# Two-layer graph network on one core: stores of the first groups moved to GpSimd's queue, four of eleven row tables on VectorE, the last norm by tiles between row parts, the last product by rows with its stores on two queues

## The reference, cut to what matters

```python
xn = layernorm(x)
x = x + rgcn_gate(xn, edges, types) + performer_attention(xn)     # layer 0
x = x + quantised_ffn(layernorm(x))
xn = layernorm(x)
x = x + gcn(xn, edges) + linear_attention(xn)                     # layer 1
# the last part, which the change touches most:
h = layernorm(x)
probs = sigmoid(h @ Wr.T + rb)                # 8 experts, best 2 kept, as weights cw
out = expert_shared(h)                        # silu(h Wg.T) * (h Wu.T) @ Wd.T
for e in range(8): out = out + cw[..., e:e+1] * expert_e(h)
x = x + out
```

## Time and profile before

| | |
|---|---|
| median of three runs | 2032.35 us |
| the profiled execution | 2033.57 us |
| its span, first to last instruction | 2032.1 us |
| TensorE busy, mean granted clock | 92% of the span, 0.958 |
| VectorE, GpSimd, ScalarE busy | 54%, 35%, 22% |
| DMA moved | 162.63 MB, mean 80 GB/s |

### The profile page before, as it was taken

One profiled execution on the slowest core, in us unless ns is written; L12 is line 12 of the kernel. 1 busy time (PEld: TensorE's weight loads), 2 busy tenths in 40 slices (PEclk: granted clock), 3 DMA queues, 4 the chain that ended last, 5 costly groups with the idle time before them and its releaser, 6 DMA issues.

```text
span 2032.1 us, 28436 instructions
## 1 busy us (share of the span) xinstructions
PE 1861.5 (92%) x9601; PEld 1456.3 (72%) x9601; DVE 1089.6 (54%) x2672; ACT 452.1 (22%) x1044; POOL 712.1 (35%) x581
## 2 busy tenths in 40 slices
PE   6989899999999999999999997544999999979997
PEld 4865566666877878778787776443878888757776
DVE  7877799998354453544534289866522234241021
ACT  3149955552011010110101130121000011010010
POOL 2000000002534535345353568000566551526651
PEclk9999999999999999999999999755999999989999
DMA  4431122222412122121224341000244441112211
GB/s 137 142 109 58 65 72 68 73 88 75 136 51 77 52 64 83 48 77 52 66 80 142 106 133 59 15 32 6 93 149 149 127 132 34 53 36 74 77 57 56
DMA packets 109418, 162.63 MB, mean 80 GB/s; under 512 B 7563, under 2 KB 42313, under 8 KB 109060
## 3 DMA queue, kind: packets, MB, share of 16 engines
q1 hardware_dynamic: 76934, 123.36, 19.8%
q10 hardware_dynamic: 32094, 36.94, 5.5%
q0 software_dynamic: 288, 1.02, 0.2%
HBM read 136.01 MB, written 25.28 MB: 79 GB/s over the span
## 4 chain that ended last, share of the span: by engine, by line
PE 66%; DVE 9%; DVEq 2%; ACT 1%; issue 1%; ACTq 0%
PE ps L409 16%; PE ps L410 16%; PE ps L411 16%; PE ps L1235 8%; PE ps L2144 1%; PE ps L1200 1%; PE ps L1642 1%; DVE stats L313 1%; PE ps L1172 1%; PE ps L1145 1%; PE ps L871 1%; DVE x L1538 0%; DVE x L1482 0%; PE ps L2155 0%; PE ps L1210 0%
## 5 line engine op out<-in xcount | busy, mean ns | idle before, releaser
L409 PE MATMUL ps<-w_hi,xt_hi 128*125 128x512 f32 (+1 forms) x1800 | 753.0, 418 | 28.8 <-DVE ring L480 7.7
L249 POOL TENSOR_TENSOR w_hi<-w_stage,zero 128x512 fp32r<-128x512 f32 x280 | 314.3, 1123 | 1240.3 <-PE ps L411 736.2
L410 PE MATMUL ps<-w_lo,xt_hi 128*125 128x512 f32 (+1 forms) x1800 | 711.5, 395 | 0.0
L411 PE MATMUL ps<-w_hi,xt_lo 128*125 128x512 f32 (+1 forms) x1800 | 709.7, 394 | 0.0
L409 PEld LDWEIGHTS ps<-w_hi,xt_hi 128*125 128x125 f32 x1800 | 338.2, 188 | 107.7 <-issue 17.0
L411 PEld LDWEIGHTS ps<-w_hi,xt_lo 128*125 128x125 f32 x1800 | 337.4, 187 | 84.9
L252 POOL TENSOR_TENSOR w_lo<-w_stage,w_hi 128x512 fp32r<-128x512 f32 x280 | 387.2, 1383 | 21.9
L410 PEld LDWEIGHTS ps<-w_lo,xt_hi 128*125 128x125 f32 x1800 | 338.3, 188 | 69.9
L1235 PE MATMUL ps<-a_hi,xn_hi 125*128 125x313 f16 (+1 forms) x640 | 106.7, 297 | 1.0 <-DVE mtmp L1373 1.0
L1235 PE MATMUL ps<-a_hi,xn_lo 125*128 125x313 f16 (+1 forms) x640 | 106.3, 296 | 0.0
L1406 DVE TENSOR_TENSOR nat<-nat,ps 125x512 f32<-125x512 f32 x80 | 51.9, 684 | 94.7 <-PE ps L411 78.8
(11 more groups left out here) (366 smaller groups left out, 2052.8 us busy)
## 6 DMA issues: line engine op xcount, KB each, us to landing
w_stage<-in_stream SPq DMA_DIRECT2D x374, 256.0 KB, 2.7
pre<-ring ACTq DMA_DIRECT2D x75, 250.0 KB
a_qk<-pre SPq DMA_DIRECT2D x16, 312.5 KB
a_qkf<-pre ACTq DMA_DIRECT2D x14, 312.5 KB
a_vx<-pre SPq DMA_DIRECT2D x9, 312.5 KB
nat<-pre SPq DMA_DIRECT2D x2, 1250.0 KB
x<-in_x SPq DMA_DIRECT2D x5, 500.0 KB
z<-pre SPq DMA_DIRECT2D x2, 1250.0 KB
```

What stands on the lines that cost most here:

```text
L249: POOL.tensor_tensor(w_hi[:, q, :], w_stage[:, q % NST, :], zero[:].to_broadcast([128, 512]), ALU.add).then_inc(S("hi_done"), 1)
L409: PE.matmul(dst, l_hi, r_hi, start=first, stop=False)
L410: PE.matmul(dst, l_hi, r_lo, start=False, stop=False)
L411: return PE.matmul(dst, l_lo, r_hi, start=False, stop=last)
```

## The change

1. `store` leaves ScalarE; GpSimd issues the 45 stores of groups 0 to 8 behind its first eight chunks. The semaphores of the stores no longer start at 16.
2. `row_on_dve`: j % 3 == 1, that is j = 1, 4, 7 and 10 of the 11.
3. The last norm: the second projection group runs in passes over tiles (0, 1) and (2, 3, 4), the turns of tiles 0 and 1 inside the second pass; the first group of the experts in passes (0, 1), (2, 3), (4,), with the turns of tiles 2, 3 and 4, the router's halves and the turning of the logits between. `meet` and `ln_split` are gone; the `again_*` helpers become `tile_*` with other banks.
4. The last product: in the second half, expert 0 for all tiles, then tile by tile experts 1 to 8. The last tile is added and stored in two halves of 256 columns; stores alternate between SyncE's and ScalarE's queue.

```diff
+    for g in range(G_PRE0 - 1):
+        for m in range(T):
+            POOL.wait_ge(S("bank_free"), (g + 1) * T + m + 1)
+            POOL.dma_start(pre[g, m], ring[:, m, :]).then_inc(S(f"stpre0_{m}"), 16)
 ...
-        def store(g):
-            for m in range(T):
-                ALE.wait_ge(S("bank_free"), (g + g0 + 1) * T + m + 1)
-                ALE.dma_start(pre[bass.ds(g, 1), m].rearrange("a p f -> p (a f)"), ring[:, m, :]).then_inc(S(f"st{tag}_{m}"), 16)
 ...
-                DVE.wait_ge(S(f"st{tag}_{m}"), 16 * g + 16)
+                if g:
+                    DVE.wait_ge(S(f"st{tag}_{m}"), 16 * g)
 ...
     def row_on_dve(j):
-        return j % 4 == 3
+        return j % 3 == 1
 ...
+    def tile_banks(m, o):
+        if m % 2 == 0:
+            return (6, 7) if o == AGAIN else (5, 6)
+        return (4, 5) if o == AGAIN else (7, m)
 ...
+    def dense_part(c0, g0, rows, behind):
+        for k in range(KT):
+            PE.wait_ge(S("split_done"), NST + c0 + k + 1)
+            for m in rows:
+                if k == 0:
+                    PE.wait_ge(S("bank_free"), g0 * T + m + 1)
+                last = three(...)
+                ...
+            behind(k)
 ...
-    dense_pe(1, C_P1, G_P1)
+    def beside_last(k):
+        if k in (3, 5):
+            tile_turn(k // 4, LAST)
+    dense_part(C_P1 + KT, G_P1 + 1, (0, 1), lambda k: None)
+    dense_part(C_P1 + KT, G_P1 + 1, (2, 3, 4), beside_last)
 ...
-    meet()
-    ln_split(x1, nat)
 ...
+    for m in (0, 1):
+        proj1_evac(1, m)
+        tile_var(m, LAST)
+    for m in (0, 1):
+        tile_norm(m, LAST)
+        tile_high(m, LAST)
+    for m in (0, 1):
+        tile_low(m, LAST)
+    for m in (2, 3):
+        proj1_evac(1, m)
+        tile_var(m, LAST)
+    for m in (2, 3):
+        tile_norm(m, LAST)
+    proj1_evac(1, 4)
+    tile_var(4, LAST)
+    for m in (2, 3):
+        tile_high(m, LAST)
+        tile_low(m, LAST)
+    tile_norm(4, LAST)
+    tile_high(4, LAST)
+    router_copy(0)
+    tile_low(4, LAST)
+    router_copy(1)
 ...
+    def beside_up(rows):
+        def behind(k):
+            if rows[0] == 0 and k in (4, 6):
+                tile_turn(2 if k == 4 else 3, LAST)
+            if rows[0] == 2 and k == 0:
+                tile_turn(4, LAST)
+            if rows[0] == 2 and k == 3:
+                PE.wait_ge(S("x_low"), LAST + T)
+                router_pe(1)
+            if rows[0] == 2 and k == 6:
+                PE.wait_ge(S("logits"), 2)
+                ...
+        return behind
+    for rows in ((0, 1), (2, 3), (4,)):
+        PE.wait_ge(S("x_low"), LAST + rows[-1] + 1)
+        if rows[0] == 2:
+            router_pe(0)
+        if rows[0] == 4:
+            PE.wait_ge(S("logits"), 1)
+        dense_part(c0, g0, rows, beside_up(rows))
 ...
+    for e in range(NEXP + 1):
+        down_part(0, (e,), range(T))
+    down_part(1, (0,), range(T))
+    down_part(1, range(1, NEXP + 1), range(T))
 ...
+            cols = ((0, 512),) if (h, m) != (1, T - 1) else ((0, 256), (256, 512))
+            for f, (b, e) in enumerate(cols):
+                n_part[0] += 1
+                o = x1[:, m, h * 512 + b:h * 512 + e]
+                DVE.tensor_tensor(o, o, ps[0:P, m, b:e], ALU.add).then_inc(S("y_done"), 1)
+                eng = (ALE, SP)[n_part[0] % 2]
+                eng.wait_ge(S("y_done"), n_part[0])
+                eng.dma_start(y[m, :, h * 512 + b:h * 512 + e], o).then_inc(S("st_out"), 16)
```

More of the change, by code:

```diff
@@ L872, in hist_pe, with beside @@
                       skip_group_check=True)
-    def beside(dense, evacuate, load_bias, store):
+    def beside(dense, evacuate, load_bias):
         mk = bucket_counts(evacuate)
@@ L2197, in beside_proj1, with beside_again @@
             feed_pe(ao1, 4 + k, FEED1 + 4 + k)
[L2199 to L2214, removed]
+    tile_turn(0, AGAIN)
+    tile_turn(1, AGAIN)
+    def beside_again(rows):
+        def behind(k):
             if rows[0] == 0 and k in (1, 5):
-                again_turn(2 + k // 5)
+                tile_turn(2 + k // 5, AGAIN)
             if rows[0] == 0 and k == 2:
@@ L2219, in build @@
             if rows[0] == 2 and k == 1:
-                again_turn(4)
+                tile_turn(4, AGAIN)
+        return behind
+    for rows in ((0, 1), (2, 3), (4,)):
+        PE.wait_ge(S("x_low"), AGAIN + rows[-1] + 1)
+        PE.wait_ge(S("down_free"), 6 if rows[0] == 0 else 2 * T)
+        dense_part(c0, g0, rows, beside_again(rows))
     for g in range(1, G_PRE1):
@@ L2396, in build, with proj1_evac @@
     done["groups"] += G_PRE1 + 2
[L2398 to L2406, removed]
+    def proj1_evac(g, m):
+        wait_bank(DVE, g, m, C_P1, G_P1)
+        o = x1[:, m, g * 512:(g + 1) * 512]
+        DVE.tensor_tensor(o, o, ps[0:P, m, :], ALU.add).then_inc(S("bank_free"), 1)
         DVE.drain()
-        done["chunks"] += 2 * KT
-        done["groups"] += 2
+        stats_tile(x1, m, (g,))
+    done["chunks"] += 2 * KT
+    done["groups"] += 2
     wr = at("wr", [128, KT, NEXP], F32, R_EXTRA)
@@ L2435, in build, with router_pe @@
         DVE.tensor_copy(n[:, :, NODES:NP2], zero[:].unsqueeze(1).to_broadcast([128, KT, 1]))
-    mk_wr = sig(DVE.drain(), "dve_step")
-    meet()
-    ln_split(x1, nat)
-    wait(PE, mk_wr)
-    for i, (h0, hn) in enumerate(((0, 314), (314, 312))):
+    H_ROUTER = ((0, 314, 4), (314, 312, 7))
+    def router_pe(i):
+        h0, hn, bank = H_ROUTER[i]
         for k in range(KT):
-            t_ = three(ps[0:NEXP, 5 + i, 0:hn], wr_hi[:, k, :], wr_lo[:, k, :], xt_hi[:, k, h0:h0 + hn], xt_lo[:, k, h0:h0 + hn],
+            t_ = three(ps[0:NEXP, bank, 0:hn], wr_hi[:, k, :], wr_lo[:, k, :], xt_hi[:, k, h0:h0 + hn], xt_lo[:, k, h0:h0 + hn],
@@ L2446, in build, with router_copy @@
                        k == 0, k == KT - 1)
-        mk = sig(t_, "pe_step")
-        wait(DVE, mk)
-        mk_lg = sig(DVE.tensor_copy(lgt[:, h0:h0 + hn], ps[0:NEXP, 5 + i, 0:hn]), "dve_step")
+        t_.then_inc(S("router"), 1)
+    def router_copy(i):
+        h0, hn, bank = H_ROUTER[i]
+        DVE.wait_ge(S("router"), i + 1)
+        DVE.tensor_copy(lgt[:, h0:h0 + hn], ps[0:NEXP, bank, 0:hn]).then_inc(S("logits"), 1)
+    for m in (0, 1):
+        proj1_evac(1, m)
+        tile_var(m, LAST)
@@ L2453, in build, with behind @@
     c0, g0 = done["chunks"], done["groups"]
[L2455 to L2462, removed]
+    def beside_up(rows):
+        def behind(k):
+            if rows[0] == 0 and k in (4, 6):
[7 more added lines that the diff above has]
+                PE.wait_ge(S("logits"), 2)
+                for t in range(T):
+                    t_ = PE.transpose(ps[0:P, 5, t * NEXP:(t + 1) * NEXP], lgt[:, t * P:(t + 1) * P], ident[0:NEXP, 0:NEXP])
+                t_.then_inc(S("router"), 1)
+        return behind
@@ L2463, in build @@
+    for rows in ((0, 1), (2, 3), (4,)):
+        PE.wait_ge(S("x_low"), LAST + rows[-1] + 1)
[4 more added lines that the diff above has]
+        dense_part(c0, g0, rows, beside_up(rows))
     with PE.Fori(1, G_UP) as g:
         dense_pe(g, c0, g0)
-    DVE.wait_ge(S("router"), 1)
-    DVE.tensor_tensor(pr[:], ps[0:P, 7, 0:T * NEXP].rearrange("p (t e) -> p t e", t=T),
+    DVE.wait_ge(S("router"), 3)
+    DVE.tensor_tensor(pr[:], ps[0:P, 5, 0:T * NEXP].rearrange("p (t e) -> p t e", t=T),
@@ L2540, in build, with down_part @@
     y = out.rearrange("(t p) d -> t p d", p=P)
-    for h in range(2):
-        for e in range(NEXP + 1):
-            c = c0 + h * (NEXP + 1) + e
-            q = c % NSL
-            PE.wait_ge(S("split_done"), NST + c + 1)
-            for m in range(T):
+    def down_part(h, experts, rows):
+        for m in rows:
+            for e in experts:
+                c = c0 + h * (NEXP + 1) + e
+                q = c % NSL
+                if m == 0:
+                    PE.wait_ge(S("split_done"), NST + c + 1)
                 if e == 0:
```

154 lines of the change are left out of this document (59 added, 95 removed).

## The result

The changed kernel takes 1986.03 us (median of 4 runs, 1983.74 to 1987.83) where the kernel before takes 2032.67 (4 runs); ratio 0.9767, 95% interval [0.9755, 0.978]. That is 46.6 us less; 38.8 were forecast and 1993.6 us. The profiled execution took 1984.67 us with a span of 1983.3, 48.8 less than the span of before.

A forecast was written before the change was run, and what follows sets the result against it. TensorE was busy 92% of the span, so only its waits counted. Terms 9.3 + 8.9 − 1 + 15.4 + 6.2 = 38.8 took the profiled 2033.57 to 1994.8, the runs to 1993.6 us; range 1983 to 2008.

The forecast's parts named there:

- Row tables, 9.3: Scatter groups: ScalarE loses two scalings a step, so 6.14 us a step instead of 6.72, 16 × 0.58 = 9.3 us less.
- TensorE's 5.85: Scatter groups: TensorE would need about 5.85 us a step, so ScalarE still leads at 6.14.
- Stores, 8.9 less 1: Group ends: stores on GpSimd's queue free ScalarE's bias load and count copies, 8.9 us gained, 1 us lost to contention.
- The 1 us of contention: Scatter and histogram groups: GpSimd's store issues hold up VectorE, taken as 1 us from a range of nothing to 18.
- The fourth rival: More than computed: granted clock stays at 1.00 after waits, steps fall to 5.85; 9 us more, 1984 us; chance 0.12.
- Last norm, 15.4: End of first projection group to logits' slot given back: 84.9 us becomes 68.9, less 0.65 lost, 15.4 us gained.
- The third rival: Last norm late tile by tile through port waits and ScalarE's order, 2 us each, 10 less gained, 2003.6 us; chance 0.13.
- Last product, 6.2: Kernel's end: tail behind the last matmul 4.3 us instead of 10.8; gain 6.4, less 0.2 for halves, 6.2 us.
- First and second rival: First: VectorE paces scatter, ScalarE's 0.58 not had, 2002.9 us, chance 0.12. Second: GpSimd's stores slow VectorE's tables, 2038.6, 0.03.
- signs: What the trace would show, among it splits 6.1 us apart and no ScalarE idle over 3 us at group ends.

The follow-up runs named there:

- e6: The changed kernel with five row tables of eleven on VectorE (j = 1, 3, 5, 7, 9) instead of four: 1986.82 us, ratio 0.9769 to the kernel before.
- e9: The changed kernel with VectorE's low part of the chunk behind the tables of j = 7 instead of j = 4: 1980.3 us, ratio 0.9748 to the kernel before.
- e3: The kernel before, stores still on ScalarE's queue, those of the last scatter and three histogram groups spread one behind each count copy 3 to 7: 2022.47 us, ratio 0.9943.
- e2: The kernel before with only the stores of groups 0 to 8 moved to GpSimd's queue: 2016.37 us, ratio 0.9918.
- e4: The kernel before with the last product alone changed (second half tile by tile, stores on two queues, last one in halves): 2026.77 us, ratio 0.996.
- e7: The changed kernel with the last tile's two stores cut by rows, 112 on one queue and 13 on the other: 1985.61 us, ratio 0.9765 to the kernel before.
- e8: The changed kernel with the last tile added and stored in one piece of 512 columns: 1986.22 us.
- e1: The kernel before with the row tables alone changed (j = 1, 4, 7 and 10 on VectorE): 2024.83 us, ratio 0.9953.
- e5: The kernel before with the last norm alone changed (by tiles between the row parts): 2016.89 us, ratio 0.992.
- e11: The changed kernel with the low parts of the histogram groups' 32 chunks made by GpSimd instead of VectorE: 2007.19 us, ratio 0.9882 to the kernel before.

## Why the prediction came out as it did

Between the two profiled executions 48.8 us came off, 10.0 more than the 38.8. Of these, 6.2 are the stores, whose term was too small, and 3.2 lie in two stretches that the change does not touch.

- **Row tables, 9.3: right.** 6.13 us a step where 6.14 stood. The reason was half right. ScalarE led, but 0.64 us a step of VectorE's wait for the split, which I took for slack, was part of the loop that held ScalarE too (0.24 a step of its own waiting, before and after; the prediction had about 0.35). e6 and e9 showed it: moving one more scaling bought nothing, moving the wait bought 0.35 a step. TensorE's 5.85 was wrong, it can do 5.62.
- **Stores, 8.9 less 1: the mechanism right, the term too small.** By place: 1.2, 1.9, 0.5 against 1.5, 2.0, 0.9 measured; and the three ends of the histogram, 2.1, 1.6 and 1.6, against 4.0, 3.3 and 2.6 (from evacuation to evacuation, and from the last to the split at 478). The six add up to 14.3; the changed execution was 0.1 us behind when they began. The step that failed is "I take 2.1, 1.6 and 1.6, between the 1.06 of TensorE and 2.15 of VectorE": I read one wait of one engine at each end. VectorE paces that part, so every wait of it counts, and behind the 2.15 there was a second:

```profile
372.15 0.49 DVE L854 TENSOR_TENSOR adj<-adj,counts 125x626 int16 x1 [1.00 <-ACT counts L845]
```

  The view puts this one down to a count copy too, but the copy that this addition reads had ended at 370.39 and VectorE came free at 371.14; a register load stands ahead of the addition in its program. What held it is not shown. In the changed kernel the same addition, at 351.15, has no wait. The waits view has the total, 11.9 us; e3 and the changed kernel returned what they took out of it, e2 1.4 us more. The 1 us of contention was not seen: over the histogram the two kinds of tables take 0.386 and 0.253 us on average, and 0.388 and 0.254 in e3, whose stores are all on ScalarE's queue (0.381 and 0.247 before). A store lands in 3.9 us by the page of the profile.
- **The clock.** TensorE's half clock behind the ends of the histogram is part of that same sum, not another one: VectorE leads there, and a slower TensorE shows as longer waits of VectorE for counts. In the profiled execution of e4, whose code is there that of before, the clock stays at 0.50 from 368 to 372 us, where before has 1.00; e4 falls 1.5 us behind, and VectorE's waits for counts are 4.5 there instead of 3.1. Where TensorE leads, the half clock costs all of it. At 1956 us of before and 1915 after, TensorE stands the same 2.41 us; before, it then ran at 0.57 for 4 us, after at 1.00, and that is the 1.6 us at 1947 to 1962:

```profile
1958.00:1962.00 4.00, 4.00 (x12) 3.11 (x11) 0.00 (x0) 0.00 (x0) 0.00 (x0) 0.57 0.00 0
```

```profile
1917.00:1921.00 4.00, 4.00 (x19) 3.21 (x18) 0.00 (x0) 0.00 (x0) 1.04 (x1) 1.00 0.00 0
```

  At this very stall e7 and e8, whose code is there the changed kernel's, lose 2.8 us to it (e7: 0.50 over 4 us and 0.64 over the next 4). So these 1.6 us are luck of the execution and not the change's. The other 1.6 arise between 1100 and 1450 us; over the same stretch, and with before's code there, the profiled executions of e1 to e5 gain between -0.1 and 1.9 us on before. So a gain of this size comes without the change; what makes it was not looked at further. The fourth rival (clock stays up, steps of 5.85) was right on the clock at two of the three ends in the histogram and wrong on the steps. The half clock behind such an end lasts longer than the 2 to 3 us that the prediction read: the mean over 4 us is 0.57 to 0.62.
- **Last norm, 15.4: right**, 15.7 in the whole change and in e5 alone. The third rival's mechanism is there: beside GpSimd's splits VectorE's small operations on two inputs (TENSOR_TENSOR, 125x1) took 0.72 to 1.06 instead of 0.16 and a norm 1.46 instead of 0.81. It took 3.0 us from tile 0, just the slack that the forecast gave it, and that it was not more is luck: the turn stood at 1783.7 less the 25.1 gained by then, 1758.6, and came at 1758.67 with a wait of 0.19. Tile 1's came at 1763.75 for 1763.6. The stall ahead of the router was 1.07 for 1.2. One step of the working does not give its figure, 28.9 less 0.65 is 28.25 and not 28.0; the next group of before takes 27.9 (1849.14 to 1877.06), so the 28.0 was right.
- **Last product, 6.2: right**, 6.4; 4.3 us behind the last matmul, as worked out, and a DMA share of 0.32, five engines, for both halves. The rule of the largest divisor, which the prediction cites from the Trainium skill, agrees with e7: 0.32 with 125 rows, 0.91 with 112.
- **First and second rival**: ScalarE's 0.58 was had in full; the stores on GpSimd's queue cost VectorE nothing that the traces show. Most of their issues fall in evacuations (346.34 to 349.37 in one from 345.36 to 348.44), so this says little of stores issued in the midst of tables. e11 shows that it is GpSimd's arithmetic that holds VectorE.
- Of the signs, one was wrong: ScalarE still idles 3.3 us at group ends. It waits for TensorE there, and nobody waits for it.

## What to carry to other kernels

Find the engine that paces a stage first, and cost a removed hold by all waits of that engine in the stage, not by the first one behind the hold. When two engines wait for each other once a step, neither is full: move the hand-over before moving work. A queue of DMA issues in the program of a compute engine costs by where it stands; spread, the same issues were nearly free (e3).

## What was not expected of the hardware

- Five stores issued in a row on ScalarE's queue took 4.2 us; the same stores one at a time, 0.28 us each (e3).
- Two stores of 125 rows on ScalarE's and SyncE's queues reached a DMA share of 0.32, cut in 112 + 13 rows 0.91 (e7). While five GpSimd stores landed it was 0.90 (350 to 352 us), with weight loads beside them; no run separates the two.
- The same 2.41 us stall of TensorE is followed by half clock in one execution and by full clock in another, a toss for 1.5 us, or for 2.8 where the half clock lasts longer. The profiled executions of e7 and e8 are 3.0 us apart at the split that comes at 141 us, in code that is the same in both; half of it arises behind one stall of 2.08 us at 113 to 115 us, after which the clock is 0.57 in e7 and 1.00 in e8. So part of what separates the runs of one kernel is this toss.
